# A routed feed-forward kernel: first block gathered by copies, b2 brought in by the tensor engine in the last stage

## What is computed

```
x = x + xattn(layernorm(x), ctx)
z = layernorm(x)                                   # per batch 64 x 128
rw = softmax(mean_over_tokens(z) @ Wr + br);  the two largest, softmax again -> weights cw
h  = gelu(z @ W1[e] + b1[e]);  expert_out = h @ W2[e] + b2[e]
y  = sum_e cw[e] * expert_out[e] + z
x  = x + layernorm(y) * gamma + beta
```

## Time and profile before

| | us |
|---|---|
| median of 3 runs | 637.44 (635.75 to 637.48) |
| the profiled execution, its own time | 637.03 |
| span of its trace | 635.2 |
| PE busy | 578.2 (91%) |
| DVE busy | 526.4 (83%) |
| ACT busy | 498.8 (79%) |
| POOL busy | 459.6 (72%) |

### The profile page before, as it was taken

One profiled execution on the slowest core, in us unless ns is written; L12 is line 12 of the kernel. 1 busy time (PEld: TensorE's weight loads), 2 busy tenths in 40 slices (PEclk: granted clock), 3 DMA queues, 4 the chain that ended last, 5 costly groups with the idle time before them and its releaser, 6 DMA issues.

```text
span 635.2 us, 19482 instructions
## 1 busy us (share of the span) xinstructions
PE 578.2 (91%) x4737; PEld 380.8 (60%) x4737; DVE 526.4 (83%) x1473; ACT 498.8 (79%) x1131; POOL 459.6 (72%) x815
## 2 busy tenths in 40 slices
PE   4899999999999999999999726999999999999762
PEld 2455555555555555555555414787888788887652
DVE  3889898988989898989898756888888888897576
ACT  3587888888887878787888627888888898887595
POOL 5788999999999999999989654656655555564233
PEclk9999999999999999999999958999999999999787
DMA  3010100010010101010020011122312332322034
GB/s 101 27 35 11 35 25 23 18 33 25 10 32 25 33 8 33 25 33 8 17 74 2 2 34 53 52 80 79 95 58 61 89 92 61 93 62 63 21 118 147
DMA packets 55583, 30.03 MB, mean 47 GB/s; under 512 B 4856, under 2 KB 54528, under 8 KB 55552
## 3 DMA queue, kind: packets, MB, share of 16 engines
q1 hardware_dynamic: 55120, 29.47, 15.8%
q10 hardware_dynamic: 432, 0.20, 0.1%
HBM read 13.00 MB, written 4.19 MB: 27 GB/s over the span
## 4 chain that ended last, share of the span: by engine, by line
PE 83%; ACT 6%; issue 4%; DVE 3%; POOL 2%; ACTq 1%; DVEq 1%; DMA 0%; POOLq 0%
PE scores_banks L350 12%; PE bank_pair L361 12%; PE bank_pair L374 7%; PE bank L387 6%; PE scores_banks L346 6%; PE scores_banks L479 5%; PE scores_banks L480 5%; PE scores_banks L481 5%; PE bank_pair L492 5%; PE bank_pair L493 5%; PE bank_pair L494 5%; PE bank L334 3%; PE bank L323 2%; ACT squares L697 2%; PE bank L327 2%
## 5 line engine op out<-in xcount | busy, mean ns | idle before, releaser
L1064 POOL TENSOR_TENSOR probs<-probs,row_sum_recip 128x512 f32<-128x512 f32 x128 | 133.6, 1044 | 19.7 <-DVE row_sum_recip L785 17.7
L586 ACT ACTIVATE probs<-scores_shifted 128x512 f32<-128x512 f32 x128 | 80.8, 632 | 52.1 <-DVE scores_shifted L779 50.7
L676 ACT ACTIVATE gelu<-scores_banks,b_expert 128x512 f32<-128x512 f32 x144 | 98.6, 691 | 26.6 <-PE scores_banks L481 19.7
L1113 POOL CAST gathered<-z_hi_lo (+1 forms) x114 | 45.9, 438 | 88.8 <-PE scores_banks L481 79.2
L769 DVE TENSOR_REDUCE row_max<-scores_banks 128x8 f32<-128x512 f32 x128 | 87.5, 684 | 24.3 <-PE scores_banks L350 24.1
L772 DVE TENSOR_REDUCE row_sum<-probs 128x8 f32<-128x512 f32 x128 | 87.1, 680 | 17.2 <-ACT probs L586 17.1
L895 DVE SCALAR_TENSOR_TENSOR zT_then_yT<-bank_pair,slot_weight,zT_then_yT x288 | 74.8, 283 | 17.2 <-issue 15.8
L595 ACT ACTIVATE probsT<-bank_pair 128x512 f32<-128x512 f32 x128 | 76.2, 595 | 14.5 <-PE bank_pair L361 13.5
L779 DVE TENSOR_TENSOR scores_shifted<-scores_banks,row_max 128x512 f32<-128x512 f32 x128 | 86.9, 679 | 0.0
L361 PE MATMUL bank_pair<-ident,probs 128*128 128x128 f32 x512 | 83.9, 286 | 2.0 <-POOL probs L1064 1.6
L350 PE MATMUL scores_banks<-k_by_head,qT 32*64 32x256 f32 x1024 | 85.5, 403 | 0.0
(11 more groups left out here) (169 smaller groups left out, 1168.7 us busy)
## 6 DMA issues: line engine op xcount, KB each, us to landing
gathered<-z_hi_lo SPq DMA_DIRECT2D x187, 64.0 KB, 1.8
x_res<-in_x SPq DMA_DIRECT2D x16, 256.0 KB, 2.6
ctxT_pair<-in_ctxT SPq DMA_DIRECT2D x32, 128.0 KB, 2.0
w_raw<-in_w SPq DMA_DIRECT2D x16, 256.0 KB, 3.0
out<-gelu SPq DMA_DIRECT2D x16, 256.0 KB, 2.2
gathered<-z_hi_lo ACTq DMA_DIRECT2D x3, 64.0 KB, 1.9
wq<-in_wq SPq DMA_DIRECT2D x1, 64.0 KB, 2.3
wk<-in_wk SPq DMA_DIRECT2D x1, 64.0 KB, 2.1
```

Of the source, the lines that this page charges most:

```text
L676: nc.scalar.activation(G[:, c, :], bank[c][:, :], ACT.Gelu, bias=b1e).then_inc(a_g if c == 0 else a_gp, 1)
L1064: nc.gpsimd.tensor_tensor(pp, pp, RC[:, k % 2, :].unsqueeze(2).to_broadcast([128, 8, S]), ALU.mult).then_inc(g_norm, 1)
```

## The change

- **First block.** The five transfers into half 0 of XG go. ACT copies batches 0 to 2 (`ACG` = 3), POOL batches 3 to 7. SP issues only the transfers of the second block.
- **b2.** `add_b2`, the DVE adds and the POOL adds go. PE multiplies B2C by CEN once, which gives the centred b2 with batches on partitions; ACT copies it to B2T. After the last block's second layer SP moves B2T, 8 transfers of 16 rows each, into eight partitions of GH (seen as B2R, in F32): 32q + half holds the rows of 16 batches. In the last stage each bank begins with a product of two partitions by 512 columns (HALF times B2R), onto which the four products with CEN accumulate. HALF is a new constant that POOL makes between steps(0) and steps(1). CEN is made at the start and not in the routing.
- **Two blocks or more for each expert.** MAXBLK goes from 39 to 44, so SLOTS from 328 to 368. The data already has two blocks or more for every expert, so the 36 blocks stay.
- **Order.** Of the eight idle products three are left. The first blocks' waits, B1E and DVE's register loads move ahead. One `x_plus_beta` on POOL is taken ahead of the loop.

```diff
-MAXBLK = (2 * NB + (GB - 1) * E) // GB
+MAXBLK = max(min((2 * NB + (GB - 1) * (E - few)) // GB, (E - few) * NB // GB) + 2 * few for few in range(E - 1))
...
+        B2R = GH[:, :, :].bitcast(F32)
...
-            b = slot_batches(mybir.EngineType.SP, 0, ACG, SPG - ACG)
-            for k in range(ACG, SPG):
-                sp.dma_start(XG[:, 0, k, :, :].bitcast(F32),
-                             Z2[:, bass.ds(b[k - ACG], 1), :, :].bitcast(F32)).then_inc(d_x0, 16)
+            sp.wait_ge(g_const, 6)
             gather(1, slot_batches(mybir.EngineType.SP, 1, 0, SPG))
...
+            sp.wait_ge(a_b2t, 1)
+            sp.wait_ge(p_l2, FC * (bounds[E] + 1))
+            sp.nop().then_inc(s_go, 1)
+            for q in range(4):
+                for half in range(2):
+                    p = 32 * q + half
+                    sp.dma_start(B2R[p:p + 1, :, :].rearrange("o c (m d) -> o (c m) d", m=4),
+                                 B2T[p:32 * q + 32:2, :]).then_inc(d_b2[q], 16)
...
-            for n in range(4):
+            pe.wait_ge(a_b2, 1)
+            pe.wait_ge(v_cen, 1)
+            nc.tensor.matmul(bank[5][:, 128:256], B2C[:, :], CEN[:, :], start=True, stop=True).then_inc(p_b2, 1)
+            for n in range(3):
                 nc.tensor.matmul(bank[3][:, 0:128], ident[:, :], ones[:, :], start=True, stop=True)
...
             for n in range(NT // 4):
-                k = n % 4
+                k, pair = n % 4, slice(32 * (n // 4), 32 * (n // 4) + 2)
+                if k == 0:
+                    pe.wait_ge(d_b2[n // 4], 32)
                 ge(pe, v_sc, n - 3)
+                nc.tensor.matmul(bank[k][:, :], HALF[pair, :, :].rearrange("p b q -> p (b q)"), B2R[pair, k, :],
+                                 start=True, stop=False, skip_group_check=True)
...
             for k in range(ACG):
-                act.dma_start(XG[:, 0, k, :, :].bitcast(F32),
-                              Z2[:, bass.ds(b[k], 1), :, :].bitcast(F32)).then_inc(d_x0, 16)
-            add_b2(range(8 * VB2 + 12, 8 * AB2))
...
+                nc.scalar.activation(XG[:, 0, k, :, :], Z2[:, bass.ds(b[k], 1), :, :].rearrange("p o j q -> p (o j) q")
+                                     .bitcast(F32), ACT.Copy).then_inc(a_x0, 1)
+            act.wait_ge(p_b2, 2)
+            nc.scalar.activation(B2T[:, :], bank[5][:, 128:256], ACT.Copy).then_inc(a_b2t, 1)
...
+            for q in range(0, 128, 32):
+                keep(HALF[q:q + 32, :, :], ALU.is_equal, 0, [[-1, 2], [0, S]], 1)
...
-            gather(0, slot_batches(mybir.EngineType.Pool, 0, SPG, GB - SPG))
+            b0 = slot_batches(mybir.EngineType.Pool, 0, ACG, GB - ACG)
+            for k in range(ACG, GB):
+                nc.gpsimd.tensor_copy(XG[:, 0, k, :, :], Z2[:, bass.ds(b0[k - ACG], 1), :, :].bitcast(F32)
+                                      ).then_inc(g_x0, 1)
```

More of the change, by code:

```diff
@@ L113, in build @@
         CEN = sb("centring", [128, 128])
+        B2T = sb("b2_rows", [128, D])
+        HALF = sb("half_of_tile", [128, 2, S])
         NE1 = sb("expert_counts", [E, 4])
@@ L210, in build @@
                                                        sem("p_second_layer"), sem("v_combined"))
-        p_b2, a_b2, a_b2y, v_b2, g_b2 = sem("p_b2"), sem("a_b2"), sem("a_b2_added"), sem("v_b2_added"), sem("g_b2_added")
+        p_b2, a_b2, a_b2t, d_b2 = sem("p_b2"), sem("a_b2"), sem("a_b2_rows"), [sem(f"d_b2_rows{q}") for q in range(4)]
         v_cen, p_y, a_sqp, a_sq, a_sd3, v_rs3, v_scp, v_sc, v_out, g_out = (
@@ L463, in _ @@
             nc.tensor.matmul(J1[:, 0:SLOTS], ones[:, :], OH[:, 1, :], start=True, stop=True).then_inc(p_r, 1)
-            for n in range(4):
-                nc.tensor.matmul(bank[3][:, 0:128], ident[:, :], ones[:, :], start=True, stop=True)
             def first_layer(n, parity, par, c):
@@ L471, in first_layer @@
                     if isinstance(n, int):
-                        pe.wait_ge(d_x0, 16 * SPG)
+                        pe.wait_ge(a_x0, ACG)
+                        pe.wait_ge(g_x0, GB - ACG)
                     else:
                         pe.wait_ge(d_xg, 16 * SPG * n)
-                    pe.wait_ge(g_xg, (GB - SPG) * (n + 1))
+                        pe.wait_ge(g_xg, (GB - SPG) * n)
                 pe.wait_ge(a_g, FC * n + (c + 1))
@@ L643, in _ @@
             nc.scalar.activation(RV[:, 15:16], RV[:, 8:9], ACT.Gelu)
-            def add_b2(batches):
-                for b in batches:
-                    yt = YT[:, S * b:S * b + S]
-                    nc.scalar.activation(yt, yt, ACT.Identity, bias=B2C[:, b:b + 1]).then_inc(a_b2y, 1)
+            act.nop().then_inc(a_g, FC)
             act.wait_ge(p_b2, 1)
@@ L802, in _ @@
             nc.vector.memset(VM[:, :, :, :, :, :], 0.0).then_inc(v_setup, 1)
+            nc.vector.tensor_scalar(CEN[:, :], ident[:, :], -1.0 / D, None, ALU.add).then_inc(v_cen, 1)
             dve.wait_ge(d_w, 64)
@@ L869, in _ @@
                                            ALU.mult, ALU.add).then_inc(v_r, 1)
+            nc.vector.tensor_copy(B1E[:, 0, :], B1A[:, 0, :]).then_inc(v_b1, 1)
+            dve.nop().then_inc(v_gl, 3)
+            dve.nop().then_inc(v_c, 2 * GB)
+            dve.nop().then_inc(v_w, 1)
             dve.wait_ge(p_r, 4)
@@ L872, in _ @@
                                            ALU.add, ALU.add).then_inc(v_r, 1)
+            bounds = expert_bounds(mybir.EngineType.DVE)
             dve.wait_ge(v_r, 6)
@@ L906, in split_lo @@
                                         ALU.subtract).then_inc(v_w, 1)
-            dve.nop().then_inc(v_gl, 3)
-            dve.nop().then_inc(v_c, 2 * GB)
-            dve.nop().then_inc(v_w, 1)
-            nc.vector.tensor_copy(B1E[:, 0, :], B1A[:, 0, :]).then_inc(v_b1, 1)
-            nc.vector.tensor_scalar(CEN[:, :], ident[:, :], -1.0 / D, None, ALU.add).then_inc(v_cen, 1)
-            dve.wait_ge(a_b2, 1)
-            for n in range(VB2):
-                yt = YT[:, 512 * n:512 * n + 512].rearrange("p (b q) -> p b q", q=S)
-                nc.vector.tensor_tensor(yt, yt, B2Y[:, 8 * n:8 * n + 8].unsqueeze(2).to_broadcast([128, 8, S]),
-                                        ALU.add).then_inc(v_b2, 1)
             dve.wait_ge(v_r, 7)
-            dve.wait_ge(v_st, 1)
-            bounds = expert_bounds(mybir.EngineType.DVE)
+            dve.wait_ge(g_const, 6)
             for e in range(E):
                 split_gelu(bounds[e])
-                if e == 0:
-                    dve.wait_ge(v_b2, VB2)
-                    dve.wait_ge(a_b2y, 8 * (AB2 - VB2))
-                    dve.wait_ge(g_b2, NB // 8 - AB2)
                 if e > 0:
@@ L1079, in _ @@
             steps(0)
-            fill((ones[:, :], 1.0), (before[:, :], 1.0), (bcol[:, 1:2], -1.0), (CWT[:, :], 0.0))
+            fill((ones[:, :], 1.0), (before[:, :], 1.0), (HALF[:, :, :], 1.0), (bcol[:, 1:2], -1.0), (CWT[:, :], 0.0))
             keep(before[:, :], ALU.is_gt, 0, [[1, 128]], -1)
+            for q in range(0, 128, 32):
+                keep(HALF[q:q + 32, :, :], ALU.is_equal, 0, [[-1, 2], [0, S]], 1)
             link(nc.gpsimd.iota(IOT[:, 0:1], pattern=[[0, 1]], base=-NOBATCH, channel_multiplier=1))
@@ L1130, in assist @@
                 nc.gpsimd.tensor_tensor(GL[:, 3, :], G[:, 3, :], GH[:, 3, :], ALU.subtract).then_inc(g_gl, 1)
-            with pool.Fori(0, NP) as g:
+            x_plus_beta(NP - 1)
+            with pool.Fori(0, NP - 1) as g:
                 assist(g)
                 x_plus_beta(g)
-            with pool.Fori(NP, blocks) as g:
+            with pool.Fori(NP - 1, blocks) as g:
                 assist(g)
```

22 lines of the change are left out of this document (8 added, 14 removed).

## The result

| | us |
|---|---|
| changed kernel, median of 4 runs | 667.17 (666.32 to 667.73) |
| kernel before, same chip, median of 4 | 636.60 (635.05 to 637.48) |
| ratio | 1.0479, 95% interval 1.0456 to 1.0503 |
| span of the changed kernel's trace | 665.6 |

A forecast was written before the change was run, and what follows sets the result against it. PE's chain was taken to bound the kernel until the last stage, where ACT's does. 637.03 + 1.1 - 3.3 + 3.1 = 637.9, plus 0.41 for the median: 638.3 us, range 635.6 to 640.5.

The forecast's parts named there:

- The b2 product in each bank: Last stage: an F32 two-row product per bank, 1.74 us at low clock, 0.86 at full, delays ACT: +3.1 us.
- the first rival: Last stage: the b2 product is cheap, 0.3 us by L350, and ACT's work covers most; 635.8 us, chance 0.13.
- The rival with the low clock: Last stage: PE becomes the bound as the low clock returns twice for three us each; 640.6 us, chance 0.15.
- The bound of 6.5: Last stage: upper bound of the b2 product's cost, with the clock rival included, +6.5 us.
- B2T into GH: Ahead of the last stage: the two awaited b2 transfers land before DVE's last combine ends; 0 us.
- a loss of that kind: Ahead of the last stage: if the b2 transfers took 1 us longer, 0.5 us would be paid.
- First block: Experts' start: copies replace transfers and ACT's adds go, so first gelu and second block come earlier: -3.3 us.
- SLOTS: Routing: 328 to 368 columns make the slot indices 0.6 us later, counted inside the first block's term.
- HALF on POOL: Attention: a memset and four selects take POOL 1.7 us, of which 1.1 reaches PE: +1.1 us.

The follow-up runs named there:

- run 9: Changed kernel with 18 full-depth F32 products filling PE's idle time ahead of the last stage, two-row b2 product still F32: 658.40 us.
- run 2: Changed kernel with each two-row b2 product replaced by one of the same length, 128 rows deep (identity by yT, output wrong): 638.43 us, ratio 1.0015.
- runs 12: Kernel before, first block copied, b2 still added to yT; no POOL adds during the slot work, DVE reads the experts' bounds while its adds run: 634.57 us.
- 13: Kernel before, first block copied, b2 in yT, no POOL adds during DVE's selects, two of POOL's four add blocks moved ahead of its gathers: 633.86 us.
- the first of 14: Changed kernel without the b2 product, HALF not filled, centring matrix made in the routing again; output lacks b2: 634.32 us, ratio 0.9946.
- run 11: Kernel before, first block copied by POOL and ACT, b2 still added to yT, five of POOL's add blocks while it waits for the indices: 640.55 us.
- runs 8: Changed kernel with the two-row product in F32R and the first four banks' b2 products issued together ahead of the first centring products: 639.89 us, ratio 1.0039.
- 10: Changed kernel with the two-row product in F32R and 18 full-depth products filling PE's idle time ahead of the last stage: 639.02 us, ratio 1.0021.

## Why the prediction was wrong, by its steps

- **The b2 product in each bank, +3.1: this step failed.** Its words were "At full clock a bank is 0.97 + 0.86 = 1.83", from "PE is at 1.2 GHz for its first six us". It carried the granted clock that this stage had in the kernel before over to a stage with other products in it. The runs showed 0.50 through all 64.16 us in its place, and the stage grew by 31.3 us. The price was also too low. By itself the product takes 2.0 us at the low clock against 1.74 by L323, and at the full one 1.05 from start to start (run 9) against 0.86; and the centring products behind it are dearer too, so that a bank is 2.14 us at the full clock and not 1.83, which is more than ACT's 2.04: PE would have been the bound even there. The cheap product of the first rival, 0.3, is excluded. With products of 128 rows (run 2) L323's 0.86 is exact (600.32 to 601.18), and the whole kernel took 638.43, the forecast, by errors that cancel.
- **The rival with the low clock** had the right quantity in view (a bank of 3.83 at the low clock against ACT's 2.04; measured 4.0), and was taken to last three us, twice, with a chance of 0.15. It was argued away by PE being busy, "hardly a pause in which the clock could fall". PE was busy 64.14 of 64.16 us at 0.50. The bound of 6.5 for this step should have been 16 banks by 3.83 less ACT's 16 by 2.04, 29 us, from the prediction's own two numbers. The Trainium skill, TensorE: Matmul & The Clock Gate, What's actually happening, ties the clock to how busy PE has been; by this case's traces busy in the profile's sense does not do: at 64 rows the clock stayed at 0.50, at 128 it rose, with PE busy in both.
- **B2T into GH, 0:** 0.54 was paid. The transfers were not slow (1.9 us in the middle); SP issued the first at 591.62, 1.2 us after PE's last product, since it first waited until its own last gather had landed; and issuing took 0.63 us each (5.06 for eight), so 1.3 for the two that PE waits for and not 0.5 to 0.9. The prediction had named a loss of that kind, for slower transfers. Small, and real.
- **First block, -3.3:** right. From the end of the attention to the last second-layer product it is 224.48 us before and 221.22 after, -3.26. First gelu 4.62 us after the indices in the changed kernel, and 4.63 to 4.67 in runs 12, 13 and the first of 14. It has two parts. PE's first layer comes 3.61 us after the indices instead of 5.59, by the copies, and the first gelu 1.01 us after PE's start instead of 2.59, since ACT's adds no longer hold it. That it was they that held it is argued from the earlier trace rows; no run has the one part without the other. Runs 12 and 13 show that the adds can be dealt so that the gain is kept, run 11 that they can be dealt so that it is lost.
- **SLOTS, +0.6:** 0.51, from the last transposition of z to the indices (18.58, now 19.09).
- **HALF on POOL, +1.1:** right. The four selects took 1.36 us. The last transposition of z begins at 367.55 to 367.67 in the three kernels without HALF and with the slow first power, and at 368.44 to 368.91 in ten of the eleven with both; in the eleventh (run 9) at 367.17, for which I have no reason. The other 0.8 of the attention's 1.86 goes with that slow first power, whose cause is open.

What stays open: whether the clock follows the depth itself or the late weight load that comes with it, for which a run is missing that has one without the other; why one short two-row product for each bank suffices to hold the low clock, why in runs 8 and 10 the clock, once up, fell at 620 and at 610 and not sooner or later, and depths between 64 and 128, which were not tried.

## What to carry to other kernels

The clock of a stage depends on the products in it: when an edit puts single products of 64 rows or fewer between full-depth ones, price the whole stage at 1.2 GHz as one of the cases, however busy PE is. Products of few rows alone don't do it. In the attention of the kernel before, products of 32 rows stand between full-depth ones for some 350 us, four of them side by side in different rows of the array, and the clock is 1.00 (a window and one group of it):

```profile
100.00:200.00 100.00, 99.10 (x1070) 54.95 (x1068) 89.68 (x252) 82.34 (x195) 91.20 (x166) 1.00 0.08 25
...
101.12 0.66 PE L350 MATMUL scores_banks<-k_by_head,qT 32*64 32x256 f32 x8
```

If such products are needed, put them together and leave the full-depth ones in one piece, or fill the rows with zeros to 128 (both raised the clock here; only the second kept it up for nearly all of the stage). And before a second engine is given vector work for free, look at what DVE does in the same microseconds.

## What the runs showed of the hardware that I had not expected

- F32 products of 512 columns and 2, 32 or 64 rows, alternating with full-depth ones, left the granted clock at 0.50 for 64 us in which PE counts as busy throughout; with 128 rows, 120 of them zero, it rose.
- The same amount of work took 646.75 or 639.89 us by the order of the products of its first four banks.
- Behind a product of fewer than 128 rows the weights of the next full-depth one were loaded only when it was over. Each change of depth took about 0.3 us more at the low clock and 0.2 at the full one, which does not show as idle time.
- POOL's adds of 512 columns beside DVE's F32 operations in SBUF stretched the latter from 0.39 to 0.93 and from 0.50 to 1.22 us.
